# First layer's attention: values in 32 columns for four heads side by side, and the softmax sums from key tiles added on GpSimd

## The reference, cut to what matters

```python
scores = jnp.einsum('bqhrd,bkhd->bhrqk', q, k) * scale
scores = jnp.where(causal, scores, jnp.finfo(scores.dtype).min)
probs = jax.nn.softmax(scores, axis=-1)
y = jnp.einsum('bhrqk,bkhd->bqhrd', probs, v)      # v = v_lat @ wv_up, v_lat has 32 numbers
x = _layernorm(x + y @ wo)
x = _layernorm(x + fp4_linear(silu(fp4_linear(x, w_gate)) * fp4_linear(x, w_up), w_down))
# second layer: attention of 16 heads in 4 groups, not causal, head size 8; then 8 gated experts
```

## Time and profile before

| | |
|---|---|
| median of 3 runs | 1389.36 us (1385.19 to 1390.56) |
| the profiled execution | 1391.06 us, span of its trace 1389.3 us |
| TensorE busy | 1263.5 us (91%) |
| VectorE busy | 1065.4 us (77%) |
| ScalarE busy | 822.1 us (59%) |
| GpSimd busy | 141.0 us (10%) |
| mean granted clock of TensorE | 0.94 of full speed |

### The profile page before, as it was taken

The page is one execution under the profiler, slowest core; times in us unless marked ns, Lnnn a source line. Parts: engine busy times, 40 slices in busy tenths (PEclk is TensorE's granted clock), DMA queues, the critical chain, the costliest instruction groups (busy, mean ns, idle before and its releaser), DMA issues.

```text
span 1389.3 us, 19169 instructions
## 1 busy us (share of the span) xinstructions
PE 1263.5 (91%) x6358; PEld 555.3 (40%) x6358; DVE 1065.4 (77%) x2275; ACT 822.1 (59%) x1625; POOL 141.0 (10%) x259
## 2 busy tenths in 40 slices
PE   5689989999999954789999999999999999999895
PEld 3345445445443432433333443343343333334333
DVE  4667886898654558678898898999889999899524
ACT  3234436455555421178888666787666787678772
POOL 5110111103020120100000002000012000000030
PEclk8669989999999986689999999999999999999997
DMA  4010100010000000000000000000000000000000
GB/s 105 21 27 22 25 1 3 22 24 1 1 1 1 1 1 0 0 1 1 1 1 1 1 1 8 1 1 1 1 1 8 1 2 1 1 1 2 1 1 16
DMA packets 10740, 10.86 MB, mean 8 GB/s; under 512 B 2857, under 2 KB 7521, under 8 KB 10641
## 3 DMA queue, kind: packets, MB, share of 16 engines
q1 hardware_dynamic: 9632, 8.84, 2.6%
q0 software_dynamic: 1008, 0.79, 0.3%
HBM read 3.66 MB, written 1.05 MB: 3 GB/s over the span
## 4 chain that ended last, share of the span: by engine, by line
PE 70%; DVE 17%; ACT 5%; issue 5%; POOL 1%; SPq 1%; DMA 1%; DVEq 0%; POOLq 0%; ACTq 0%
PE ps L850 23%; PE ps L831 14%; PE ps L740 9%; DVE MP L1315 8%; PE ps L827 6%; PE ps L745 4%; ACT PR L1059 3%; PE ps L803 2%; PE ps L736 2%; PE ps L769 2%; PE ps L705 1%; DVE ps L1312 1%; PE ps L751 1%; PE ps L780 1%; DVE ST L1237 1%
## 5 line engine op out<-in xcount | busy, mean ns | idle before, releaser
L1059 ACT ACTIVATE PR<-ps 128x512 f32<-128x512 f32 (+2 forms) x1344 | 698.8, 586 | 381.7 <-PE ps L827 193.4
L1315 DVE TENSOR_REDUCE MP<-ps 128x1 f32<-128x512 f32 x1216 | 761.9, 683 | 118.1 <-PE ps L740 69.9
L850 PE MATMUL ps<-PR,V 128*32 128x512 f32 (+2 forms) x2688 | 433.7, 601 | 3.1 <-ACT OS L937 2.5
L740 PE MATMUL ps<-KO,Q 64*128 64x512 f32 x1024 | 379.9, 459 | 14.2 <-DVE MP L1315 7.3
L831 PE MATMUL ps<-Q,KO 64*128 64x512 f32 x1024 | 343.7, 446 | 10.2 <-DMA Q<-MR 6.0
L831 PEld LDWEIGHTS ps<-Q,KO 64*128 64x128 f32 x1024 | 160.2, 186 | 297.4 <-issue 128.4
L740 PEld LDWEIGHTS ps<-KO,Q 64*128 64x128 f32 x1024 | 170.4, 189 | 90.1 <-DVE MP L1315 35.9
L745 PE MATMUL ps<-KO,QO 96*128 96x512 f32 (+2 forms) x320 | 124.3, 436 | 23.0 <-DVE QO L1296 10.0
L827 PE MATMUL ps<-QO,KO 97*128 97x512 f32 (+3 forms) x320 | 140.3, 454 | 4.1 <-DMA QO<-MR 2.4
L850 PEld LDWEIGHTS ps<-PR,V 128*32 128x32 f32 (+1 forms) x2688 | 74.1, 115 | 128.2 <-issue 61.4
L827 PEld LDWEIGHTS ps<-QO,KO 97*128 97x128 f32 x320 | 61.0, 197 | 130.9 <-issue 80.3
(11 more groups left out here) (211 smaller groups left out, 772.3 us busy)
## 6 DMA issues: line engine op xcount, KB each, us to landing
QO<-Q SPq DMA_DIRECT2D x72, 64.0 KB, 2.0
Q<-MR SPq DMA_DIRECT2D x64, 2.0 KB
result<-V SPq DMA_DIRECT2D x4, 256.0 KB, 2.3
H<-in_L_attn_wq SPq DMA_DIRECT2D x1, 512.0 KB, 3.4
HQT<-in_L_attn_wo SPq DMA_DIRECT2D x1, 512.0 KB, 5.8
ew<-in_L_ffn_expert_w POOLq DMA_DIRECT2D x1, 512.0 KB, 4.2
bq<-in_L_attn_bq POOLq DMA_DIRECT2D x12, 0.1 KB, 3.4
wd<-in_L_ffn_w_down SPq DMA_DIRECT2D x1, 176.0 KB, 4.8
```

The source lines that it names most:

```text
L740: last = nc.tensor.matmul(bank[:, :], Q1[rows, buf, h // 2, q * P:(q + 1) * P], KO1[rows, g, kc * QC:(kc + 1) * QC], start=True, stop=True)
L850: nc.tensor.matmul(dst, VO[layer][:, kt, g, :], PR[:, u % NP_RING, q0:QC], start=kt == 0, stop=kt == key_tiles(layer, c) - 1).then_inc(pv_ ...
L1059: nc.scalar.activation(PR[:, u % NP_RING, q0:QC], ps[:, bank_of_score[u], q0:QC], ACT.Exp, scale=SCALE[layer]).then_inc(exp_done, 1)
L1315: v.tensor_reduce(MP[:, buf, h, q, kc:kc + 1], bank[:, 0:w], AX, ALU.max).then_inc(free, 1)
```

## The change

- `V0` has 32 columns and no ones. The four heads of a key tile are multiplied side by side, into bank 4 alone, all four at one place in the order (they came two by two).
- The softmax sums go to bank 5, each 32 times over, by new `sums` steps: a matmul of `ones_v` (128x32 ones) with a sum of two key tiles of probabilities. GpSimd makes these in `add_tiles`, in four buffers `SUMS`: two in `PS`, two in the space of `ew`. Heads 0 and 1 pair tiles (0,1), (2,3) and so on; heads 2 and 3 take tile 0 alone (a copy by ScalarE at kt = 1, by GpSimd in chunk 0), then (1,2), (3,4), and the last tile by a matmul with ones of its own. There is one buffer a head: GpSimd waits on `sums_done` before it overwrites, and ScalarE on `paired` before it reuses a place in the ring.
- `out0` of the sums is a matmul with four columns of the identity in place of a transpose; VectorE takes one reciprocal and one multiply in place of two each.
- `ew` is loaded by SP once the last sums are done.

```diff
-        V0 = sb("V0", [P, NT, G0, VW0])
+        V0 = sb("V0", [P, NT, G0, LAT])
+        ones_v = sb("ones_v", [P, LAT])
+        PS = sb("PS", [P, HG - 2, QC])
+        SUMS = [PS[:, 0, :], PS[:, 1, :], flat(ew[:, 0:NE // 2, :]), flat(ew[:, NE // 2:NE, :])]
+        def added(step):
+            _, layer, c, _, _, kt, h = step
+            if layer == 1:
+                return []
+            if kt % 2 == h // 2 or kt == 0 and c:
+                return []
+            return [kt - 1, kt] if kt else [kt]
...
-                    yield from carry + out_copies(urgent)
+                    yield from [s for s in carry if s[0] == "products"] + out_copies(urgent[-1:])
                 else:
+                    if slot == HG + pause:
+                        yield from [s for s in carry if s[0] == "sums"] + out_copies(urgent[:-1])
                     n, m = len(late), slots - HG
                     yield from late[n * (slot - HG) // m:n * (slot - HG + 1) // m]
-                    if (slot + 1) % SIDE_BY_SIDE[layer] == 0:
-                        for h in range(slot % HG + 1 - SIDE_BY_SIDE[layer], slot % HG + 1):
-                            yield ("products", layer, c, g, it, slot // HG - 1, h)
+                    if slot % HG == HG - 1:
+                        kt = slot // HG - 1
+                        for h in range(HG):
+                            yield ("products", layer, c, g, it, kt, h)
+                        if layer == 0 and kt % 2:
+                            yield ("sums", c, g, kt // 2)
...
+                            if step[2:] == (0, 0):
+                                sp.wait_ge(sums_done, sum(HG for s in steps if s[0] == "sums"))
+                                sp.dma_start(ew[:, :, :], A["L1_ffn_expert_w"].rearrange("e k n -> k e n")).then_inc(ld["experts"], 16)
...
+                elif kind == "out0" and item[1] == 1:
+                    for q in range(QT):
+                        last = nc.tensor.matmul(bank[:, q * HG:(q + 1) * HG], OS[:, 1, q * P:(q + 1) * P], ident[:, 0:P:WIDE],
+                                                start=True, stop=True)
...
+            def sums(step, outs):
+                _, c, g, p = step
+                if p == 0 and outs:
+                    pe.wait_ge(out_free, outs)
+                if p == 0 and c:
+                    copies_at[0] += HG // 2
+                    pe.wait_ge(copied, copies_at[0])
+                pe.wait_ge(paired, added_at.pop(step))
+                for h in range(HG):
+                    q0 = first_query(0, c, max(0, 2 * p - h // 2))
+                    nc.tensor.matmul(ps[h * WIDE:(h + 1) * WIDE, OUT_BANKS[1], q0:QC], ones_v[:, :], SUMS[h][:, q0:QC],
+                                     start=p == 0, stop=2 * p + 2 == key_tiles(0, c)).then_inc(sums_done, 1)
...
+                        if layer == 0 and c and kt == 1 and h >= HG // 2:
+                            act.wait_ge(sums_done, sums_at[0] - HG + h + 1)
+                            act.wait_ge(exp_done, n.units + u - HG + 5)
+                            copy(SUMS[h], PR[:, (u - HG) % NP_RING, :]).then_inc(copied, 1)
...
+                        if u - NP_RING in added_by:
+                            act.wait_ge(paired, added_by[u - NP_RING])
...
+            def add_tiles(unit, c, kt, h, adds, groups, clips):
+                tile = lambda n: PR[:, (unit - HG * n) % NP_RING, :]
+                q0, into = first_query(0, c, kt), SUMS[h]
+                done = HG * (groups - 1) + h + 1
+                if done > 0:
+                    pool.wait_ge(sums_done, done)
+                if diagonal(0, c, kt):
+                    pool.wait_ge(clipped, clips)
+                else:
+                    pool.wait_ge(exp_done, unit + 5)
+                if kt == 0:
+                    nc.gpsimd.tensor_copy(into, tile(0)).then_inc(paired, 1)
+                    return
+                before = first_query(0, c, kt - 1)
+                if before < q0:
+                    nc.gpsimd.affine_select(into[:, before:q0], tile(1)[:, before:q0], [[1, P]], ALU.is_ge, nothing, base=0,
+                                            channel_multiplier=-1)
+                nc.gpsimd.tensor_tensor(into[:, q0:QC], tile(1)[:, q0:QC], tile(0)[:, q0:QC], ALU.add).then_inc(paired, 1)
...
-            v.memset(V0[:, :, :, :], 1.0).then_inc(stored, 16)
+            v.memset(ones_v[:, :], 1.0).then_inc(stored, 16)
```

More of the change, by code:

```diff
@@ L37 @@
 LOWEST = -3e38
-VW0, VW1 = 64, 32
+VW1 = 32
+WIDE = P // HG
 EXPONENT = 0x7f800000
@@ L179, in build @@
         ROW = ((6, 7, 0, 1, 2, 3), (5, 6, 7, 0, 1, 2, 3))
-        ld = {n: sem("loaded_" + n) for n in ("x", "query", "keys", "attn0", "ffn0", "attn1", "moe", "const", "masks")}
+        ld = {n: sem("loaded_" + n) for n in ("x", "query", "keys", "attn0", "ffn0", "attn1", "moe", "experts", "const", "masks")}
         side_full = sem("side_full")
@@ L239, in outs0 @@
         def outs0(c, g):
-            return [("out0", b, c, g) for b in range(2)]
+            return [("out0", b, c, g) for b in (1, 0)]
         def gaps(text, steps):
@@ L360, in iteration @@
             late[at:at] = urgent
+            pause = max(i for i in range(2) if len(late) * i // (slots - HG) <= at)
             for slot in range(slots):
@@ L378, in last_products @@
         def last_products(layer, c, g, it):
-            return [("products", layer, c, g, it, key_tiles(layer, c) - 1, h) for h in range(HG)]
+            kt = key_tiles(layer, c) - 1
+            return ([("products", layer, c, g, it, kt, h) for h in range(HG)]
+                    + ([("sums", c, g, kt // 2)] if layer == 0 else []))
         def stream(part, with_queries=True):
@@ L499, in is_side @@
         def is_side(step):
-            return step[0] not in ("scores", "products") + BANKLESS
+            return step[0] not in ("scores", "products", "sums") + BANKLESS
         def name_of(item):
@@ L874, in walk @@
                         continue
+                    if kind == "sums":
+                        sums(step, outs)
+                        continue
+                    if kind == "scores" and added(step):
+                        adds_at[0] += 1
+                        if step[5] % 2:
+                            added_at["sums", step[2], step[3], step[5] // 2] = adds_at[0]
                     for name in needs(step):
@@ L917, in walk @@
                         pe.wait_ge(ld["attn1"], N_ATTN1)
-                        pe.wait_ge(ld["moe"], 64)
+                        pe.wait_ge(ld["moe"], 48)
+                    if kind == "expert":
+                        pe.wait_ge(ld["experts"], 16)
                     if kind == "wgT":
@@ L1064, in walk @@
                             pv_at[0] = pv_seen(steps, step)
+                    elif kind == "sums":
+                        sums_at[0] += HG
                     elif kind == "out_copy":
-                        act.wait_ge(pv_done, n.units + NP_RING - lag + pv_at[0])
+                        if len(step) > 2 and step[1] == 1:
+                            act.wait_ge(sums_done, sums_at[0])
+                        else:
+                            act.wait_ge(pv_done, n.units + NP_RING - lag + pv_at[0])
                         bank = OUT_BANKS[step[1] if len(step) > 2 else 0]
@@ L1150, in walk @@
             def walk(steps, n, lag):
-                k, rs, tiles, tails, units = 0, 0, 0, 0, 0
+                k, rs, tiles, tails, units, adds, clips, groups = 0, 0, 0, 0, 0, 0, 0, 0
+                tile = []
                 for step in steps:
@@ L1156, in walk @@
                             clip(n.units + units, first_query(*step[1:3], step[5]))
+                            clips += 1
+                        tile.append((units, step))
+                        if not diagonal(*step[1:3], step[5]) or step[6] % 2:
+                            for unit, (_, layer, c, _, _, kt, h) in tile:
+                                if added(("scores", layer, c, 0, 0, kt, h)):
+                                    add_tiles(unit, c, kt, h, adds, groups + kt // 2, clips)
+                                    adds += 1
+                            if kt == key_tiles(layer, c) - 1 and h == HG - 1:
+                                groups += kt // 2 + 1
+                            tile = []
                         units += 1
@@ L1462, in walk @@
                     kind = step[0]
-                    if kind in ("scores", "products", "out_copy"):
+                    if kind in ("scores", "products", "sums", "out_copy"):
                         continue
```

43 lines of the change are left out of this document (28 added, 15 removed).

## The result

The changed kernel takes 1429.53 us (median of four runs, 1425.01 to 1435.46), the kernel before 1389.15 beside it (four runs). The ratio is 1.0296, 95% interval [1.0266, 1.0326]: 40 us slower, where 20 us faster was forecast and 1388 was the upper end of the range.

What follows compares the result with a forecast made beforehand. TensorE was taken to bound the first layer's four longest stretches, with VectorE close in chunk 2's second iteration. 24 of TensorE's 38 us arrive: 1391.06 - 24 + 2.5 - 1 + 0.5 = 1369 us, range 1352 to 1388.

Steps and rivals of the forecast that it cites:

- TensorE's balance: First layer: halved products, less added sums, fewer shape changes and sums' output, leave TensorE 38 us less work.
- joined sums: First layer: a group of four matmuls with ones behind a quad costs some 0.85 us; 0.9 taken, 36 us in all.
- rival 1: First layer: all 38 us of TensorE's saving arrive, VectorE's operations slipping between the adds; 1355 us, chance 0.2.
- The sum of VectorE's loss: First layer: GpSimd's adds delay VectorE's operations between buffers, 9 us in a second iteration, 5 in a first.
- its 63.5 us stay: Chunk 2's second iteration: VectorE's load reaches 65 us, so the length stays and TensorE's 6 us are not had.
- the mean wait: Shared-port rule at its word: an operation meeting an add waits half of 1.28 us, 13 us in place of 9.
- The ring: First layer: adds wait for sums and exponentials for adds; slack over 3 us, so nothing on the path.
- Rival 3: First layer: head 2's exponential waits for an add that waits for the sums; 27 us more, about 1418; chance 0.1.
- The clock: TensorE's clock would fall if it idled; 3 us in the range for early stretches; below 1.0 in chunks 2, 3 means wrong.
- The first score of layer 1: Layer 1's start: experts' load moves ahead of the row copies it waits for; 2.5 us later (0.5 to 4.5).
- The power for the norm: Second halves in the first layer: it stands behind adds, about 1 us each, up to 2.5 in chunk 3's second.
- Rival 2: First layer: VectorE loses about twice as much, 17 us in second iterations, 8 in first; 1387 us, bound 1400; chance 0.15.

Runs made afterwards that it cites:

- experiment 1: The changed kernel with every GpSimd add cut to 32 columns and no selects, so the softmax sums lack most terms: 1373.76 us, ratio 0.989.
- Experiment 3: The changed kernel with VectorE's quantising chains made of one-input reductions (quantising left out), whole adds kept: 1395.31 us, ratio 1.0044.
- experiment 6: The changed kernel with a second buffer for the added tiles of heads 2 and 3: 1418.23 us, ratio 1.0201.
- experiments 9: The changed kernel with adds cut to 32 columns but the 48 selects before them kept: 1379.91 us, ratio 0.9907.
- experiment 7: The changed kernel with both second buffers for heads 2 and 3 and one-input reductions for VectorE's quantising chains: 1390.27 us, ratio 0.9986.
- experiment 2: The kernel before with the same GpSimd adds, on constant buffers into one that nobody reads: 1417.35 us, ratio 1.0199.
- experiment 12: The changed kernel with adds in chunk 3 alone, issued by VectorE one score tile behind, direct sums elsewhere: 1388.62 us, ratio 0.9987.

## Why the prediction was wrong

**TensorE's balance was right.** Quads take 1.00 us, joined sums 0.86 (0.9 taken). Freed of the adds' length, TensorE's busy time fell by 36.2 us (413.6 to 377.4; 38 forecast), and chunk 3's iterations by 8.6 and 11.0 us where 8.4 was all that was forecast. But the saving was taken to arrive, less what the adds cost, and it doesn't: with adds that cost next to nothing the prediction's own sum gives rival 1's 1355 us, and the kernel took 1374. That this lies near the forecast of 1369 is luck; the forecast had 14 us for the adds in it. The 19 us between are a second miss: chunk 1 gains nothing and chunk 2's second iteration loses 2.9 us (experiment 1), and 5 us are lost behind the layer, for causes that stay open.

**The sum of VectorE's loss was right, its weight was not; this is the step that failed.** I put 5 us in a first iteration and 9 in a second, 42 us over chunks 1 to 3. The excess grew by 40 us in the layer, though not as I had it by iteration: chunk 2's second has 4.7 us and chunk 3's second 12.0, so the sum is partly luck. But I let a loss count only where VectorE's busy time would come near the iteration's length, as in "its 63.5 us stay", and gave chunk 1's first iteration a gain of 3 us. That iteration got 9.8 us longer, with VectorE busy for 42.5 of 57.0. The quantising chains are serial, each operation waiting for the one before, and TensorE's transposes wait at their end: L806 8.2 us and L797 3.8, where the same transposes of the kernel before waited 3.2 (L775) and 0.4. A lengthened chain delays whoever waits for it, however idle its engine is. Experiment 3 priced it: 36 us of excess removed, 34 us of time back.

By the Trainium skill, SBUF — State Buffer, "SBUF: two separate sides", a VectorE instruction with at most one SBUF input outside the 2-port modes doesn't contend, and one with two contends with a GpSimd instruction that reads SBUF, the first to issue holding the ports for its whole length. The trace agrees: the reduction of 352 columns takes 520 ns both times, `XQ<-qa,qs` goes from 420 to 934, and an operation takes at most 1.51 us where 0.52 was usual. Half of the excess lies in `tensor_scalar` operations with one SBUF tensor; whether they ran in a 2-port mode no trace shows. The prediction used that rule only for the mean wait, 13 us in place of 9; by the excess measured, 0.2 us an operation was the better figure.

**The ring was put at nothing; it costs 5 us (with one-input chains) to 11.** ScalarE waited for adds 44 times, 34 us in all, and second buffers gave 11 us back (experiment 6). I had the adds at 1.28 us and the ring's slack at 3 us. Their means were 1373 and 1321 ns, since GpSimd is held off too, and two in a row took up to 2.95. GpSimd was busy for 44.6 of 69.1 us in chunk 3's first iteration, over the 60% that I had named as its ceiling. Rival 3 named this mechanism, its bad case 51 us; it is a fifth of that. Its 1418 us were the nearest of all to what was measured, and the signs named for it came (exponentials waiting for 34 us, clocks of 0.92, 0.91 and 0.85), but for the most part by another way: with the ring's waits nearly gone 1418 us remain (experiment 6).

**The clock.** The prediction has it under rival 3, among the signs, and with 3 us in the range; the sum of the forecast has nothing for it. TensorE ran at its low level for 47.8 us of the layer before and 112.6 us after. The same instructions then stay busy for 34 us longer than in experiment 1. That the long adds bring the low clock, and not the matmuls, follows from experiments 1 and 3, in which the same matmuls have 37.5 and 58.0 us of it; that they do so through TensorE's waits is the plain reading, not shown by itself. How many of the 40 us are the clock's share can't be separated, since no run held the clock.

**The rest.** The first score of layer 1 comes 0.8 us later behind the layer's end than before (2.5 taken, 0.5 the lower bound), the first score of the kernel 1.3 us earlier (1 taken). The power for the norm stood behind two adds in chunk 3's second iteration, 2.5 us, as the upper bound had it ("up to 2.5"). Rival 1 (1355 us) had the wrong sign for the same reason as the forecast. Rival 2 was the nearest by its mechanism, and even its bound of 1400 was too low: it, too, counted VectorE by volume.

**The account.** From the changed kernel's 1429.5 us: one-input chains -34, second buffers on top of them -5, shorter adds -10 to -16 more (experiments 9 and 1). Of this last part it stays open how much is GpSimd's queue (clips and powers behind adds), how much the ring of heads 0 and 1, which keep one buffer, and how much the contention that experiment 7 still has (10.4 us of excess, 4.2 in experiment 1).

## What to carry to other kernels

When work moves to an idle engine, ask first which operations of its neighbours it slows, and then whether those stand in a serial chain that a third engine waits for; busy shares say nothing about that. Before trusting spare time on GpSimd beside VectorE's two-input operations, put the same instructions into the old kernel with nobody waiting for them, as experiment 2 did: it showed 27 us, of the 56 between long adds and short ones. And price the gain by itself: with short adds TensorE was busy for 36 us less, and the kernel was 15 faster. Many short instructions contend less than few long ones, but each has a fixed part, so splitting helps only an engine with slack.

## What the runs showed of the hardware

- Beside 128x512 GpSimd adds of two f32 tiles, VectorE operations with two SBUF inputs go from 420 to 934 ns in the mean (256 columns) and from 520 to between 605 and 781 (352), one of 520 to 1508 at most. Reductions of one SBUF input, and operations that read PSUM, keep their means to 2 ns. `tensor_scalar` operations with one SBUF tensor are hit as much: 284 to 729 ns (256 columns), 346 to 531 for the norm, at most 1396.
- The adds pay as well: 1373 ns in the mean where 1280 is usual.
- GpSimd's f32 add takes 477 ns for 128 columns beside 1280 for 512, a select 653 for 512 and 297 for 128, an add of 32 columns 270. VectorE's add of 512 columns takes 679 to 687 (experiment 12).
- A longer layer came with a lower clock: 32 us more in the first layer went with 65 us more at TensorE's low level, and some 2100 matmul records were busy for 34 us longer than with short adds.
